# First two attention units' packed operands computed directly, modulation products in pieces, earlier weight loads, and a new instruction order

## The reference, cut to what matters

```
ada  = silu(c @ ada1_w + b) @ ada2_w + b           # 6 rows of 256 per batch
qkv  = x @ qkv_w ; 16 heads of 16
attn = softmax(where(mask, q k^T / 4, -inf)) v      # only keys that are valid
x = x + gate_msa * modulate(layernorm(attn @ proj_w + b))
x = x + gate_mlp * modulate(layernorm(gelu(x @ fc1_w + b) @ fc2_w + b))     # hidden 1024
emb = silu(c) @ ada_w + b                          # second layer, 6 rows of 256
x = x + gate * (gelu(modulate(ln(x)) @ ssm_w1) @ ssm_w2)                     # hidden 256
x = x + gate * (gelu(modulate(ln(x)) @ ff_w1) @ ff_w2)                       # hidden 512
```

## Time and profile before

| | |
|---|---|
| median of 3 runs | 416.91 us |
| the profiled execution's own time | 414.57 us |
| its span, first to last instruction | 412.8 us |
| mean granted TensorE clock | 0.907 |
| TensorE busy | 361.1 us (87%) |
| TensorE weight loads busy (beside the products) | 287.5 us (70%) |
| VectorE busy | 235.8 us (57%) |
| ScalarE busy | 226.1 us (55%) |
| GpSimd busy | 172.9 us (42%) |
| data moved by DMA | 33.28 MB |

### The profile page before, as it was taken

One profiled execution on the slowest core, in us unless ns is written; L12 is line 12 of the kernel. 1 busy time (PEld: TensorE's weight loads), 2 busy tenths in 40 slices (PEclk: granted clock), 3 DMA queues, 4 the chain that ended last, 5 costly groups with the idle time before them and its releaser, 6 DMA issues.

```text
span 412.8 us, 7527 instructions
## 1 busy us (share of the span) xinstructions
PE 361.1 (87%) x2560; PEld 287.5 (70%) x2560; DVE 235.8 (57%) x550; ACT 226.1 (55%) x431; POOL 172.9 (42%) x179
## 2 busy tenths in 40 slices
...
DMA packets 21557, 33.28 MB, mean 81 GB/s; under 512 B 2085, under 2 KB 13287, under 8 KB 21512
## 3 DMA queue, kind: packets, MB, share of 16 engines
...
...
## 4 chain that ended last, share of the span: by engine, by line
PE 69%; DVE 8%; DMA 7%; issue 6%; ACT 5%; POOL 2%; SPq 2%; ACTq 0%; DVEq 0%; POOLq 0%
PE ps L902 43%; PE ps L1020 5%; PE ps L1008 4%; PE ps L965 4%; PE ps L996 4%; PE ps L928 3%; DMA p_qa<-p_m_rows 2%; DMA pq_dram<-p_qk_buf 2%; PE ps L1027 2%; POOL p_hid L537 2%; DMA p_column<-in_columns 2%; DMA pmod_dram<-p_vec 1%; DVE p_stats L707 1%; PE ps L980 1%; ACT p_gelu L686 1%
## 5 line engine op out<-in xcount | busy, mean ns | idle before, releaser
L537 POOL TENSOR_TENSOR p_hid<-p_gelu,p_hid 128x512 fp32r<-128x512 f32 x56 | 72.9, 1306 | 80.7 <-ACT p_hid L695 80.4
L775 DVE TENSOR_REDUCE p_nmax<-ps 128x2 f32<-128x512 f32 x128 | 81.3, 680 | 27.6 <-PE ps L996 27.6
L664 ACT ACTIVATE p_probs<-ps 128x512 f32<-128x512 f32 x128 | 67.7, 607 | 33.9 <-PE ps L1008 32.5
L555 POOL TENSOR_TENSOR x_all<-x_all,p_vec 128x512 f32<-128x512 f32 x32 | 40.9, 1285 | 46.5 <-DMA x_all<-in_x 21.4
L902 PE MATMUL ps<-p_fc_hi,p_hid 128*128 128x256 f32 x256 | 51.3, 287 | 0.4 <-POOL p_hid L537 0.4
L902 PEld LDWEIGHTS ps<-p_fc_hi,p_hid 128*128 128x128 f32 x256 | 40.9, 188 | 3.0 <-POOL p_hid L537 0.9
L686 ACT ACTIVATE p_gelu<-ps,p_column 128x256 f32<-128x256 f32 x64 | 26.8, 470 | 24.9 <-PE ps L902 17.9
L1008 PE MATMUL ps<-p_qa,p_ka 51*128 51x512 f32 x128 | 32.7, 517 | 6.7 <-DMA p_qa<-p_m_rows 4.2
L686 ACT ACTIVATE p_gelu<-ps,p_upb_mod 128x256 f32<-128x256 f32 x48 | 20.0, 470 | 32.4 <-PE ps L902 31.4
L695 ACT ACTIVATE p_hid<-p_gelu 128x512 fp32r<-128x512 f32 x56 | 35.3, 634 | 3.2 <-PE ps L902 2.0
L902 PE MATMUL ps<-p_m_hi,p_fc_hi 128*128 128x256 f32 x128 | 36.8, 288 | 0.0
...
## 6 DMA issues: line engine op xcount, KB each, us to landing
...
pq_dram<-p_qk_buf SPq DMA_DIRECT2D x6, 512.0 KB, 4.8
p_vec<-pmod_dram SPq DMA_DIRECT2D x4, 512.0 KB, 5.2
...
p_probs<-in_L_cond_ada_w ACTq DMA_DIRECT2D x1, 1536.0 KB, 11.6
...
p_adb_raw<-in_L_cond_ada_w ACTq DMA_DIRECT2D x1, 1536.0 KB, 9.9
p_big_raw<-in_xT SPq DMA_DIRECT2D x2, 512.0 KB, 4.8
```

The costliest lines, as they stand in the source:

```text
L537: pool.tensor_tensor(hid[:, TOOK[of][0], 1, :], gelu_out[:, TOOK[("gelu",) + step[1:]][0], :], hid[:, TOOK[of][0], 0, :].bitcast(F32), ALU ...
L555: pool.tensor_tensor(tiles(m, h), tiles(m, h), vec[:, m // NCH, SHIFT[L], :].rearrange("p (o c) -> p o c", o=1).broadcast_to([P, 2, C]), A ...
L664: act.activation(probs[:, kt, 2 * p + e, :], ps[:, TOOK["s2", a, g, kt, p][e], :], ACT.Exp, scale=SCALE).then_inc(s_exp, 1)
L775: dve.tensor_reduce(nmax[:, u % 2, e, 0, at:at + 2], ps[:, TOOK["s1", a, g, j][e], :].rearrange("p (t n) -> p t n", t=2), axis=AX.X, op=AL ...
```

## The change

1. **Direct packed operands (units 0 and 1 of chunk 0).** The columns of the query and key weights of heads 0 to 7 are written three times over and in packed positions (`pw`, ScalarE, with the lo part in `pwlo`, VectorE), into the tiles of the `ff1` and `ff2` weights, which are not in use yet. Then `pq/p` and `pk/p` (p = 0 to 3, a pair of heads each) give the products directly on the packed rows. `pqhi`/`pkhi` (ScalarE) and `pqlo`/`pklo` (VectorE) make hi or lo of each row by a per-partition sign, the ones and the mask row included. There is no store to DRAM and no packing load for these two units; `q/0/0`, `k/0/0`, `qst/0/0`, `kst/0/0`, `qa/0/0`, `qa/0/1`, half of `ka` and `maskd` go. Units 2 and 3 are packed as before.
2. **Modulation products in pieces.** `ada/0` and `ada/1` are 4 steps of 12 such instructions each, `upb` 3 steps of 8, with other steps in between.
3. **Weights asked for early.** `ld/proj` waits for nothing and stands 11th in the order; `ld/fc1`, `ld/ssm1`, `ld/ff1` follow within the first 40 steps. Splitting `ff1` and `ff2` waits for the last `pq` and `pk`.
4. **Moved between engines.** `xlo/1/0` and `wlo/v` go from VectorE to GpSimd. The transposed x of chunk 1 is loaded in two halves, the second half first.
5. **Six more transposes at the start** (14 in place of 8).
6. **A new order** of all steps, to the end of the kernel.

The diff, cut to its core:

```diff
+PACKED = H // 4
+ADA_PARTS, UPB_PARTS = 4, 3
+EARLY = {("qhi", 0, 1): 0, ("khi", 0, 1): 1}
...
 ORDER = [...
-    xhi/0/1 xhi/0/0 xlo/0/1 whi/q xlo/0/0 wlo/q q/0/0 xhi/1/1 xhi/1/0 xlo/1/1 ada1 whi/k xlo/1/0 in/ada2 qhi/0/0 wlo/k q/0/1 qlo/0/0 masks
-    qst/0/0 k/0/0 silu q/1/0 qhi/0/1 khi/0/0 qlo/0/1 maskd whi/v klo/0/0 k/0/1 qhi/1/0 biashl kst/0/0 q/1/1 khi/0/1 qa/0/0 qlo/1/0 qst/0/1
-    ada/0 klo/0/1 wlo/v qst/1/0 ka/0/0 qa/0/1 kst/0/1 v/0/0 adaE/0 qhi/1/1 qlo/1/1 s1/0/0/0 s1/0/0/1 max/0/0/0/0 qst/1/1 s1/0/0/2
...
+    xhi/0/0 xhi/0/1 xlo/0/0 whi/q xlo/0/1 pw/q wlo/q q/0/1 xhi/1/1 pwlo/q ld/proj pw/k in/ada2 xlo/1/1 pq/0 xhi/1/0 pwlo/k whi/k ada1
+    xlo/1/0 qhi/0/1 masks pq/1 pqhi/0 whi/v wlo/v qlo/0/1 pk/0 in/proj pqlo/0 qst/0/1 q/1/0 silu biashl pqhi/1 pk/1 pkhi/0 ld/fc1 pqlo/1
+    ada/0/0 ld/ssm1 in/fc1 split/proj pklo/0 qhi/1/0 wlo/k pkhi/1 s1/0/0/0 qlo/1/0 ld/ff1 s1/0/0/1 k/0/1 max/0/0/0/0 qst/1/0 pk/2
+    max/0/0/0/1 khi/0/1 max/0/0/1/0 q/1/1 in/ff1 klo/0/1 qa/0/2 max/0/0/1/1 pk/3 pklo/1 in/ssm1 kst/0/1 qhi/1/1 split/fc1 s1/0/0/2 qlo/1/1
+    s1/0/0/3 ada/0/1 pkhi/2 max/0/0/2/0 qst/1/1 max/0/0/2/1 v/0/0 max/0/0/3/0 pq/2 ld/adb max/0/0/3/1 qa/0/3 ld/xt0 in/adb vev/0/0 ld/fc2
+    pklo/2 v/0/1 ka/0/1 pqhi/2 pq/3 pqlo/2 pkhi/3 vev/0/1 pklo/3 s1/0/1/0 pqhi/3 ada/0/2 ldxT/2 max/0/1/0/0 pqlo/3 split/ssm1 ld/ssm2
+    mT/0/0 s1/0/1/1 ld/ff2 max/0/1/0/1 ada/0/3 ld/xt1 in/ssm2 max/0/1/1/0 mhi/0/0 split/ff1 mlo/0/0 s1/0/1/2 in/xt0 max/0/1/1/1 md/0/0
+    s1/0/1/3 s1/0/2/0 max/0/1/2/0 ada/1/0 max/0/1/2/1 in/fc2 max/0/1/3/0 s1/0/2/1 xhi/2/0 ada/1/1 adaE/0 xhi/2/1 max/0/1/3/1 xlo/2/0 rT/0
+    ada/1/2 rE/0 max/0/2/0/0 mod/0 xlo/2/1 max/0/2/0/1 mT/0/1 in/ff2 s1/0/2/2 mhi/0/1 max/0/2/1/0 s2/0/0/0/0 ada/1/3 mlo/0/1 max/0/2/1/1
+    md/0/1 q/2/0 in/xt1 max/0/2/2/0 exp/0/0/0/0/0 split/fc2 vec/0 max/0/2/2/1 exp/0/0/0/0/1 adaE/1 s2/0/0/0/1 qhi/2/0 s1/0/2/3 s2/0/0/1/0
...
+    packed_w = {"q": [w[:, :, :] for w in weights["ff1"]], "k": [w[:, :, :].rearrange("p (k a) n -> p k (a n)", k=KC) for w in weights["ff2"]]}
...
+    def qk_buf_free(was):
+        if was[0] == "xlo":
+            return x_lo_done(*was[1:])
+        return (s_pq_lo, upto(*was)) if was[0] in ("pqlo", "pklo") else stored(was)
+    def packed_cols(name, part, k):
+        return packed_w[name][part][:, k, :].rearrange("p (h c) -> p h c", c=64)[:, :, 0:R_MASK].rearrange("p h (d r) -> p h d r", r=3)
+    def repeated_cols(which, k):
+        return sh.qkv_raw[:, k, which * C:which * C + 2 * PACKED * D].rearrange("p (h d o) -> p h d o", d=D, o=1).broadcast_to([P, 2 * PACKED, D, 3])
...
+            elif kind == "pw":
+                which = "qk".index(step[1])
+                act.wait_ge(sh.s_qkv_raw[which], 16)
+                for k in range(KC):
+                    act.activation(packed_cols(step[1], 0, k), repeated_cols(which, k), ACT.Identity).then_inc(s_pw, 1)
+            elif kind in ("pqhi", "pkhi"):
...
+                for was in BEFORE[step]:
+                    act.wait_ge(*qk_buf_free(was))
+                act.activation(qk_buf[:, TOOK[step][0], 0, 0:width], ps[:, TOOK[of][0], 0:width], ACT.Identity,
+                               scale=low_sign[:, which:which + 1], bias=one_rows[:, which:which + 1]).then_inc(s_pq_hi, 1)
...
-                if name == "proj":
-                    act.wait_ge(s_qa[NG - 1], 32)
-                    act.wait_ge(s_ka0[1], 32)
                 if name == "adb":
-                    for was in (("qst", 0, 0), ("qst", 0, 1), ("kst", 0, 0)):
+                    for was in (("qst", 0, 1), ("kst", 0, 1)):
                         act.wait_ge(*stored(was))
...
+            elif kind in ("pqlo", "pklo"):
...
+                dve.scalar_tensor_tensor(out=qa[:, p // PAIRS, p % PAIRS, :] if kind == "pqlo" else ka[:, p, :], in0=ps[:, TOOK[of][0], 0:width],
+                                         scalar=low_rows[:, which:which + 1], in1=qk_buf[:, TOOK[hi][0], 0, 0:width].bitcast(F32),
+                                         op0=ALU.mult, op1=ALU.subtract).then_inc(s_pq_lo, 1)
...
-        for _ in range(8):
+        for _ in range(14):
             pe.transpose(ps[:, BANKS - 1, 0:P], ident[:, :], ident[:, :])
...
+            elif kind in ("pq", "pk"):
+                p = step[1]
...
+                last = product(dst[:, 0:width], [[packed_w[kind[1]][part][:, k, p * P:(p + 1) * P] for k in range(KC)] for part in range(2)],
+                               [[act[part][:, k, at] for k in range(KC)] for part in range(2)], stop=kind == "pq")
+                if kind == "pk":
...
+                    last = pe.matmul(dst[:, 0:KEYS], mask_rows, mask_neg[0:1, :], start=False, stop=True)
...
-                n = step[1]
-                pe.wait_ge(s_silu, 3)
-                pe.wait_ge(s_ada_raw[n], 16)
-                dst, = take(step)
-                for f in range(6 * KC):
+                _, n, i = step
+                if i == 0:
+                    pe.wait_ge(s_silu, 3)
+                    pe.wait_ge(s_ada_raw[n], 16)
+                    take(step)
+                dst = ps[:, TOOK["ada", n, 0][0], :]
+                for f in range(i * 6 * KC // ADA_PARTS, (i + 1) * 6 * KC // ADA_PARTS):
```

More of the change, by code:

```diff
@@ L198, in given_back, with on_pool @@
         return last_of(("xlo", step[1], 0), ("xlo", step[1], 1))
-    return {"ada1": ("silu",), "ada": ("adaE",) + step[1:], "rT": ("rE",) + step[1:], "upb": ("upbs",)}[kind]
+    return {"ada1": ("silu",), "ada": ("adaE",) + step[1:2], "rT": ("rE",) + step[1:], "upb": ("upbs",)}[kind]
+def on_pool(a, h):
+    return a >= NCH or (a, h) == (1, 0)
 PLACE = {step: n for n, step in enumerate(ORDER)}
@@ L216, in numbered @@
         kind = step[0]
-        group = "xlo2" if kind == "xlo" and step[1] >= NCH else TOGETHER[kind] if kind in TOGETHER else kind
+        group = TOGETHER[kind] if kind in TOGETHER else kind
+        if kind == "xlo" and on_pool(*step[1:]) or step == ("wlo", "v"):
+            group += " on GpSimd"
         assert step not in at, step
@@ L222, in numbered @@
             free[what].append((thing, step))
-        if kind in TAKES and step not in EARLY and not (kind in ("pv", "dn") and step[-1] > 0):
+        if kind in TAKES and step not in EARLY and not (kind in ("pv", "dn", "ada", "upb") and step[-1] > 0):
             what, number = TAKES[kind]
@@ L527, in gpsimd @@
                 pool.tensor_tensor(lo[:, :, :], raw_tile, hi[:, :, :].bitcast(F32), ALU.subtract).then_inc(s_split, 1)
-            elif kind == "xlo" and step[1] >= NCH:
+            elif kind == "xlo" and on_pool(*step[1:]):
                 _, a, h = step
@@ L586, in scalar @@
                     act.wait_ge(s_qk_mm, max(upto("q", 1, fc) for fc in range(KC)))
-                    act.wait_ge(s_qk_mm, max(upto("k", 0, fc) for fc in range(KC)))
+                    act.wait_ge(s_qk_mm, upto("k", 0, 1))
+                    act.wait_ge(s_pq_mm, upto("pk", PACKED - 1))
                     act.wait_ge(s_v_mm, max(upto("v", 0, kt) for kt in range(KT)))
@@ L730, in vector @@
                 dve.tensor_tensor(bias_hl[32:33, :, :], bias_raw[32:33, :, :], bias_hi[32:33, :, :].bitcast(F32), ALU.subtract).then_inc(s_biashl, 1)
-            elif kind == "wlo":
+            elif kind == "wlo" and step[1] != "v":
                 n = "qkv".index(step[1])
@@ L736, in vector @@
                     .then_inc(s_qkv_lo, 1)
-            elif kind == "xlo" and step[1] < NCH:
+            elif kind == "pwlo":
+                which = "qk".index(step[1])
+                dve.wait_ge(s_pw, KC * upto("pw", step[1]))
+                for k in range(KC):
+                    dve.tensor_tensor(packed_cols(step[1], 1, k), repeated_cols(which, k), packed_cols(step[1], 0, k).bitcast(F32), ALU.subtract)\
+                        .then_inc(s_pw_lo, 1)
+            elif kind in ("pqlo", "pklo"):
+                of, hi = (kind[:2],) + step[1:], (kind[:2] + "hi",) + step[1:]
+                which, p, width = "qk".index(kind[1]), step[1], CH if kind == "pqlo" else KEYS
+                dve.wait_ge(s_pq_hi, upto(*hi))
+                dve.scalar_tensor_tensor(out=qa[:, p // PAIRS, p % PAIRS, :] if kind == "pqlo" else ka[:, p, :], in0=ps[:, TOOK[of][0], 0:width],
+                                         scalar=low_rows[:, which:which + 1], in1=qk_buf[:, TOOK[hi][0], 0, 0:width].bitcast(F32),
+                                         op0=ALU.mult, op1=ALU.subtract).then_inc(s_pq_lo, 1)
+            elif kind == "xlo" and not on_pool(*step[1:]):
                 _, a, h = step
```

357 lines of the change are left out of this document (207 added, 150 removed).

## The result

The changed kernel takes **390.08 us** (median of 4 executions, 387.96 to 393.63) against 417.09 for the kernel before: a ratio of 0.9366 [0.9281, 0.9452]. The forecast was 405, with a range from 395 to 416, so it was too slow by 15 us. Ratios here use only the executions within 1.5% of the fastest of their kernel, medians use all, so a ratio can differ by about 1% from the quotient of two medians.

The account below looks back on a forecast made before the run. TensorE bounds the kernel; the first stage loses 22.3 us to the clock and 19.2 to waits. First `O` at 20 + 62.5 + 8 = 90.5 instead of 101.8 gains 11.3: 405 us, range 395 to 416.

Parts of the forecast that it names:

- For the stage behind I take zero: After the first `O`: the new order was taken to gain or lose 0 us.
- a TensorE 96% busy: Stage behind the first `O`: the cover for taking zero; worse cover would cost 11.5 us idle again at worst.
- 11.5 us to win there at most: From 101.8 to 360 us: TensorE busy 246.65 of 258.2 us, so a better order could win only 11.5 us.
- some of the 20.9 us idle: Last stage: moving deferred chunk-2 work beside the last chunk's attention could win part of this; nothing was taken.
- I take 3: TensorE's wait for the load `ld/adb` at `ada/1/0`, ahead of the first `s2`: 0 to 5 us, taken as 3.
- the deciding point: Front, up to the first `O`: from 39 us at the low clock on, the change loses.
- The clock never falls: Rival: TensorE stays at 2.4 GHz, first `O` at 82.5, gain of 19, 398 us (394 to 400); chance 0.18.
- Given back later: Rival: front wins but the order stalls more between 100 and 360, up to 11.5 us; 413 to 420; chance 0.12.
- Slower by a low clock: Rival: clock falls at about 35 and stays low until the projections; `O` at 118, 433 us; chance 0.09.
- Stores and weights late: Rival: early weights delay the slot's store and `adb`; 5 us more idle, 411 us (409 to 412.7); chance 0.13.
- `s1` beyond 24 (operands): Sign of being wrong: first score product, forecast at 19 to 21 us, after 24, with the operands as cause.
- `ada/1/0` after 45 (weights): Sign of being wrong: first piece of `ada/1` after 45 us, with the weights as cause.

Follow-up runs that it names:

- h2: Kernel before with its own order up to the first `O` step, then the changed kernel's order: 397.97 us, ratio 0.9618.
- v1: Changed kernel with the small per-partition columns loaded by ScalarE between its two modulation weights instead of by SyncE: 390.44 us, ratio 0.9414.
- c1: Changed kernel with `ld/fc2`, `ld/xt0`, `ld/ssm2`, `ld/ff2` and `ld/xt1` asked for behind the first exponentials: 394.78 us, ratio 0.959.
- p1: Changed kernel with the pieces of `ada/0`, `ada/1` and `upb` put together again as whole products: 403.33 us.
- c2: Changed kernel with five loads moved behind the first exponentials and the pieces of `ada/1` spread behind the first `s2`: 399.65 us, ratio 0.972.
- p2: Repeat of the changed kernel with whole products for `ada/0`, `ada/1` and `upb`: 403.37 us, ratio 0.9714.
- v13b: Changed kernel, columns loaded early, `ld/ssm2`, `ld/ff2`, `ld/xt1` behind first exponentials, 20 unused transposes ahead of unit 2's wait; a repeat: 385.62 us, ratio 0.9321.
- e4: Changed kernel with `ld/ssm2`, `ld/ff2` and `ld/xt1` moved behind the first exponentials: 389.63 us, ratio 0.9417.

## Why the prediction was wrong

**The step that failed: "For the stage behind I take zero".** The stage gained 15.4 us, and h2 shows it alone: 15.4 by medians (413.32 to 397.97). With the forecast's own front, 403.3 - 15.4 = 387.9 would have been 3 us below the 391.15 profiled. Two errors stand in it, and one guess that nearly held.
- The new order was read only up to the first `O`. The prediction's cover was "a TensorE 96% busy", and it priced a loss at 11.5 us but no gain. The idle 11.55 us in the earlier trace rows were a price that a better order could win, and it won 7.2.
- The bound "11.5 us to win there at most" was too low; with the same steps in it the stage gave 12.7. It counts neither the clock's dip that follows a stall (1.8 us) nor busy time that shrinks with the same steps in it (some 3.7 us, the 1.4 of the moved step left out). What those 3.7 us are stays open: most instruction groups have the same mean durations within a few ns, but `s2` products went from 480 to 456 ns.
- That the last stage could win "some of the 20.9 us idle" but would be worth nothing was nearly right: its idle time went from 20.9 to 19.6 us, and it gained 1.3, or 2.7 with the same steps in it.

**The front, step by step.** The work was right (67.1 forecast, 67.6 measured). The first score came at 25.07 instead of 20: the load of the columns was not on the list of what stands ahead of it, and it cost 3.57 us idle and a low stretch; v1 without it has its first score at 20.20. Unit 1 came at 38.7, not 33: the store of `q/1/1` was asked for at 33.06, not near 27. The first `s2` came at 58.95, not 45. "I take 3" for the wait at `ada/1/0` was 4.1 at the products ahead of it, and from 48.79 on three pieces of `ada/1` and what lies between them took 10.2 us at half speed. The low clock was 30 us, not 16, as 12.6 us against 8; and the deciding point, 39 us low, is near what c1 (38, 394.78) and p1 (38) have: they were still far below the kernel before, because of the rest.

**The rivals.** The clock never falls: it fell twice. Given back later: the opposite happened. Slower by a low clock: the mechanism exists, as c2 and p2 show with 52 us, but not here. Stores and weights late: right in kind; moving more of the weights later gained nothing, so they did not decide. Two of the prediction's signs of being wrong, "`s1` beyond 24 (operands)" and "`ada/1/0` after 45 (weights)", both came, and the front still gained 7.9. Neither had the cause named with it: the columns held the first, the blocked issues the second.

**The two rules.** In v13b the clock fell inside a piece of `ada/1` with TensorE busy 6.50 of 6.50 us, in the kernel after inside a piece of `ada/0` with it busy 2.99 of 3.00, and in p2 inside `upb`. Both causes exist: an idle wait (at 11 to 14.7 in the kernel after, and ahead of 30.09 in v1) and dense 2-column products. The Trainium skill, "TensorE: Matmul & The Clock Gate", "Why this matters for your kernels", tells of the gap alone; the trace of the kernel after agrees with it at 14.2 us and goes beyond it at 41.7. The pieces gained although a gap-only rule gives them nothing. The Trainium skill, "DMA: Bandwidth & Descriptors", "Issuing engines are not separate DMA queues", calls the time to initiate a transfer usually small beside the transfer; here it was 9.1 us for three, and 1.5 us for the same three in e4.
